# Scores of a windowed attention from stacked rows through memory, halves straight from PSUM, reciprocals in PSUM

## The reference

```python
x = x + jnp.tanh(g_xattn[0]) * attention(_layernorm(x), ctx, ctx, wq, bq, wk, bk, wv, bv, wo, bo)
x = x + jnp.tanh(g_ffn[0]) * experts(_layernorm(x), ln_gamma, ln_beta, Wr, W12, W3)
```

```python
q = split(jnp.einsum('btc,oc->bto', query, wq) + bq) * SCALE      # SCALE = 16 ** -0.5
k = split(jnp.einsum('btc,oc->bto', key, wk) + bk)
scores = jnp.where(valid, jnp.einsum('bhnrd,bhncd->bhnrc', qb, kc), neg_inf)
out = jnp.einsum('bhnrc,bhncd->bhnrd', softmax(scores), vc)
```

## Time and profile before

| | before |
|---|---|
| median of 3 runs | 534.16 us (533.97 to 535.27) |
| profiled execution | 534.19 us |
| its span in the trace | 532.3 us |
| granted TensorE clock, mean | 0.973 |
| busy in the span: TensorE, VectorE, ScalarE, GpSimd | 90%, 68%, 56%, 39% |

### The profile page before, as it was taken

The page is one execution under the profiler, slowest core; times in us unless marked ns, Lnnn a source line. Parts: engine busy times, 40 slices in busy tenths (PEclk is TensorE's granted clock), DMA queues, the critical chain, the costliest instruction groups (busy, mean ns, idle before and its releaser), DMA issues.

```text
span 532.3 us, 10749 instructions
## 1 busy us (share of the span) xinstructions
PE 479.7 (90%) x3551; PEld 444.7 (84%) x3551; DVE 360.8 (68%) x854; ACT 298.9 (56%) x757; POOL 208.9 (39%) x272
## 2 busy tenths in 40 slices
PE   5699999899999877369998999999999999999991
PEld 4588887777877666269998999999999999999991
DVE  6867888988888997547876574485843768544240
ACT  3689878677778764416664564373723747423230
POOL 8636776787787566510212012203032030311202
PEclk9999999999999997779999999999999999999996
DMA  8868432314142611153677362347451474201111
GB/s 269 209 140 250 78 41 72 75 57 81 42 80 55 205 42 53 58 175 118 234 184 219 78 226 34 60 129 193 132 144 20 130 188 131 31 4 17 13 19 20
DMA packets 41649, 57.33 MB, mean 108 GB/s; under 512 B 3721, under 2 KB 38576, under 8 KB 39552
## 3 DMA queue, kind: packets, MB, share of 16 engines
q1 hardware_dynamic: 35168, 48.62, 31.7%
q0 software_dynamic: 6144, 8.07, 9.1%
q10 hardware_dynamic: 288, 0.00, 0.0%
HBM read 36.24 MB, written 16.72 MB: 99 GB/s over the span
## 4 chain that ended last, share of the span: by engine, by line
PE 55%; DVE 3%; issue 2%; POOL 1%; DMA 0%; ACT 0%; POOLq 0%; DVEq 0%
PE bank L1438 17%; PE bank L1440 17%; PE bank L1439 17%; PE bank L1432 2%; PE bank L1361 1%; PE bank L1304 1%; POOL expert_rows L484 0%; DMA expert_rows<-xr,slotu 0%; DVE pT L929 0%; PE bank L1290 0%; POOL out_tokens L546 0%; DVE nm L924 0%; PE bank L1231 0%; PE bank L1238 0%; DVE osum L938 0%
## 5 line engine op out<-in xcount | busy, mean ns | idle before, releaser
L546 POOL DMA_INDIRECT out_tokens<-ysc,rows x32 | 49.6, 1550 | 245.6 <-DVE ysc L1142 238.9
L1438 PE MATMUL bank<-bXh,wh 128*128 128x384 f32 (+1 forms) x384 | 122.1, 318 | 2.9 <-issue 2.6
L1440 PE MATMUL bank<-bXh,wl 128*128 128x384 f32 (+1 forms) x384 | 121.8, 317 | 0.0
L1439 PE MATMUL bank<-bXl,wh 128*128 128x384 f32 (+1 forms) x384 | 121.8, 317 | 0.0
L749 ACT ACTIVATE sil<-bank 128x384 f32<-128x384 f32 (+1 forms) x96 | 43.7, 456 | 128.4 <-PE bank L1440 127.2
L1121 DVE TENSOR_TENSOR hF<-sil,bank 128x384 f32<-128x384 f32 (+1 forms) x96 | 48.9, 510 | 77.9 <-ACT sil L749 71.3
L633 ACT ACTIVATE p<-bank,nm 128x128 f32<-128x128 f32 x256 | 73.6, 387 | 14.7 <-DVE nm L924 14.7
L1438 PEld LDWEIGHTS bank<-bXh,wh 128*128 128x128 f32 x384 | 72.7, 189 | 3.3 <-issue 3.3
L1438 PE MATMUL bank<-wh,hH 128*128 128x256 f32 x256 | 73.8, 288 | 0.3 <-DVE ysc L1142 0.3
L1439 PEld LDWEIGHTS bank<-bXl,wh 128*128 128x128 f32 x384 | 72.7, 189 | 0.0
L1440 PEld LDWEIGHTS bank<-bXh,wl 128*128 128x128 f32 x384 | 72.6, 189 | 0.0
(11 more groups left out here) (146 smaller groups left out, 878.8 us busy)
## 6 DMA issues: line engine op xcount, KB each, us to landing
stage<-in_w12T SPq DMA_DIRECT2D x16, 1024.0 KB
stage<-in_w3T SPq DMA_DIRECT2D x8, 1024.0 KB
expert_rows<-padrow SPq DMA_DIRECT2D x8, 662.5 KB, 7.9
rows<-expert_rows SPq DMA_DIRECT2D x7, 662.5 KB, 4.4
kM<-k SPq DMA_DIRECT2D x64, 64.0 KB, 2.4
cT<-in_ctxT SPq DMA_DIRECT2D x8, 256.0 KB, 3.1
out_tokens<-x_all SPq DMA_DIRECT2D x8, 256.0 KB, 2.3
x_all<-in_x SPq DMA_DIRECT2D x2, 640.0 KB, 8.5
```

What stands on the lines that cost most here:

```text
L546: pool.indirect_dma_start(out=out, out_offset=bass.IndirectOffsetOnAxis(rows[par][:, c, D + E:ROW].bitcast(U32), 0), in_=ysc[par][:, c, :] ...
L1438: nc.tensor.matmul(out_ap, ah, bh, start=start, stop=False)
L1439: nc.tensor.matmul(out_ap, ah, bl, start=False, stop=False)
L1440: return nc.tensor.matmul(out_ap, al, bh, start=False, stop=stop)
```

## The change

Four things are changed.

The scores of blocks 1 to 7. The three products are put on top of each other in rows: two heads have 32 rows, and the three pairs of halves stand in 3 x 32 = 96 rows (qS holds queries high, high, low; kS keys high, low, high). Two heads are 256 columns, so a group is two products of 256 columns over 96 rows (`scores`). Block 0 keeps the old form (`first_scores`, one kM).

The way there. Queries and keys must change rows for that. SyncE stores each half into a scratch tensor in memory (qD, kD: four stores of 256 KB a block), waits for the store, and loads from there into the stacks: six loads of 128 KB into 16 rows for the keys, three of 256 KB into 32 rows for the queries (`stack`, in place of `spread_keys`). kS is cleared once, kS[0] by VectorE, kS[1] by GpSimd.

The halves. ScalarE writes the high half straight from PSUM with the bias added, VectorE the low half straight from PSUM (`keys_low`, `queries_low`: bank plus bias less the high half), so that kT, qT, two copies by ScalarE and two subtractions by GpSimd a block go. The scale of the queries goes to the copy of the input's columns. The bank Xp is handed on in another order: keys of the next block in step 0, columns of the input in step 1, queries in step 2, values in step 6. `normalize_inputs` of GpSimd comes ahead of the first normalization.

The reciprocals of the heads' sums are written into PSUM, behind the outputs of the heads (orec).

The core of the diff (changed lines only; renamed semaphores and small edits of the start are left out):

```diff
+        qD = nc.dram_tensor("query_halves", (2, P, DC, SB * T), F32).ap()
+        kD = nc.dram_tensor("key_halves", (2, P, DC, SB * T), F32).ap()
...
-        kM = [sb(pa, f"kM{i}", [P, 2, H, SB * T], F32R) for i in range(2)]
+        kM = sb(pa, "kM", [P, 2, H, SB * T], F32R)
+        kS = [sb(pa, f"kS{i}", [P, HP, 2, SB * T], F32R) for i in range(2)]
...
-        qT = sb(pa, "qT", [P, DC, SB * T], F32)
-        q2 = [sb(pa, f"q2_{i}", [P, 2, DC, SB * T], F32R) for i in range(2)]
-        kT = sb(pa, "kT", [P, DC, SB * T], F32)
+        qS = [sb(pa, f"qS{i}", [P, HP, SB * T], F32R) for i in range(2)]
+        q0 = qS[0][:, 0:2 * DC, :].rearrange("p (s c) t -> p s c t", s=2)
+        q2 = sb(pa, "q2", [P, 2, DC, SB * T], F32R)
...
-        orec = sb(pa, "orec", [P, 8], F32)
...
+        orec = [O[i][:, 8 * VW:8 * VW + 8] for i in range(2)]
...
-            def spread_keys(n, par):
-                sp.wait_ge(pool_kl, n + 1)
+            def spread_first_keys():
+                sp.wait_ge(dve_kl, 1)
-                    sp.dma_start(kM[par][r, :, a:H:HR, :].bitcast(F32), k2[r, :, :, :].bitcast(F32)).then_inc(ld_km[a // GH], 16)
+                    sp.dma_start(kM[r, :, a:H:HR, :].bitcast(F32), k2[r, :, :, :].bitcast(F32)).then_inc(ld_km[a // GH], 16)
+            def stack_keys(par, part, half):
+                for h in range(2):
+                    r = part * SR + h * HD
+                    sp.dma_start(kS[par][r:r + HD, :, h, :].bitcast(F32).rearrange("d (c a) t -> d c a t", c=DC),
+                                 kD[half].rearrange("(a h d) c t -> h d c a t", h=2, d=HD)[h]).then_inc(ld_k, 16)
+            def stack_queries(par, part, half):
+                sp.dma_start(qS[par][part * SR:(part + 1) * SR, :, :].bitcast(F32).rearrange("r (c a) t -> r c a t", c=DC),
+                             qD[half].rearrange("(a r) c t -> r c a t", r=SR)).then_inc(ld_q, 16)
+            def stack(n, par):
+                sp.wait_ge(act_kh, DC * (n + 1))
+                sp.dma_start(kD[0], k2[:, 0, :, :].bitcast(F32)).then_inc(sent_kh, 16)
+                sp.wait_ge(dve_kl, n + 1)
+                sp.dma_start(kD[1], k2[:, 1, :, :].bitcast(F32)).then_inc(sent_kl, 16)
+                sp.wait_ge(sent_kh, 16 * n)
+                stack_keys(par, 0, 0)
+                stack_keys(par, 2, 0)
+                sp.wait_ge(sent_kl, 16 * n)
+                stack_keys(par, 1, 1)
+                sp.wait_ge(act_qh, DC * (n + 1))
+                sp.dma_start(qD[0], q2[:, 0, :, :].bitcast(F32)).then_inc(sent_qh, 16)
+                sp.wait_ge(dve_ql, n + 1)
+                sp.dma_start(qD[1], q2[:, 1, :, :].bitcast(F32)).then_inc(sent_ql, 16)
+                sp.wait_ge(sent_qh, 16 * n)
+                stack_queries(par, 0, 0)
+                stack_queries(par, 1, 0)
+                sp.wait_ge(sent_ql, 16 * n)
+                stack_queries(par, 2, 1)
...
-            sp.wait_ge(km_zero[0], 4)
-            spread_keys(0, 0)
+            sp.wait_ge(km_zero, 3)
+            spread_first_keys()
-            sp.wait_ge(km_zero[1], 3)
-            spread_keys(1, 1)
+            sp.wait_ge(ks_zero[1], 1)
+            stack(1, 1)
...
-                spread_keys(n, par)
+                    sp.wait_ge(ks_zero[0], 2)
+                stack(n, par)
...
-            keys_low(0)
+            pool.memset(kS[1][:, :, :, :].bitcast(F32), 0.0).then_inc(ks_zero[1], 1)
...
-                if nxt:
-                    keys_low(n + 1)
+                if nxt2:
+                    normalize_inputs(n + 2)
-                if nxt2:
-                    normalize_inputs(n + 2)
-                if nxt:
-                    queries_low(n + 1, 1 - par)
...
-                act.activation(xT[:, :, :], Xp[:, :].rearrange("p (c t) -> p c t", c=DC), ACT.Copy).then_inc(act_xT, 1)
-            def queries(n, par, bank, prev1):
+                act.activation(xT[:, :, :], Xp[:, :].rearrange("p (c t) -> p c t", c=DC), ACT.Copy, scale=HD ** -0.5).then_inc(act_xT, 1)
+            def queries(n, halves, bank):
-                if prev1:
-                    act.wait_ge(pool_ql, n)
+                if not (isinstance(n, int) and n < 2):
+                    act.wait_ge(sent_qh, 16 * (n - 1))
-                    act.activation(qT[:, t, :], bank[:, t * SB * T:(t + 1) * SB * T], ACT.Identity,
-                                   bias=bq4[:, t:t + 1], scale=HD ** -0.5).then_inc(act_q32, 1)
-                act.wait_ge(act_q32, DC * (n + 1))
-                act.activation(q2[par][:, 0, :, :], qT[:, :, :], ACT.Copy).then_inc(act_q, 1)
-            def keys(n, bank, prev1):
+                    act.activation(halves[:, 0, t, :], bank[:, t * SB * T:(t + 1) * SB * T], ACT.Identity, bias=bq4[:, t:t + 1])\
+                       .then_inc(act_qh, 1)
+            def keys(n, bank):
-                if prev1:
-                    act.wait_ge(pool_kl, n)
+                if isinstance(n, int) and n == 1:
+                    for half in ld_km:
+                        act.wait_ge(half, KM)
+                elif not isinstance(n, int) or n > 1:
+                    act.wait_ge(sent_kh, 16 * (n - 1))
-                    act.activation(kT[:, t, :], bank[:, t * SB * T:(t + 1) * SB * T], ACT.Identity, bias=bqkv[:, 1, t:t + 1])\
-                       .then_inc(act_k32, 1)
-                if prev1:
-                    for half in ld_km:
-                        act.wait_ge(half, KM * n)
-                act.wait_ge(act_k32, DC * (n + 1))
-                act.activation(k2[:, 0, :, :], kT[:, :, :], ACT.Copy).then_inc(act_kT, 1)
+                    act.activation(k2[:, 0, t, :], bank[:, t * SB * T:(t + 1) * SB * T], ACT.Identity, bias=bqkv[:, 1, t:t + 1])\
+                       .then_inc(act_kh, 1)
...
+                    if g == 7 and nxt:
+                        values(n + 1, Xp)
+                    if cur:
+                        exps(G, g, not prev1 and g < 2)
+                    if g == 0 and nxt:
+                        keys(n + 1, Xp)
-                    if g == 7 and nxt:
-                        values(n + 1, Xp)
-                    if g == 3 and nxt:
-                        keys(n + 1, Xp, True)
-                    if cur:
-                        exps(G, g, not prev1 and g < 2)
-                    if g == 4 and nxt:
-                        queries(n + 1, 1 - par, Xp, True)
-                    if g == 0 and nxt:
+                    if g == 2 and nxt:
+                        queries(n + 1, q2, Xp)
+                    if g == 1 and nxt:
...
-            keys(0, K0, False)
+            act.wait_ge(ident_ok, 1)
+            act.activation(kM[:, 1, :, :].rearrange("p h (a t) -> p (h a) t", t=P),
+                           ident32[:, :].unsqueeze(1).to_broadcast([P, 2 * H, P]), ACT.Copy, scale=0.0).then_inc(km_zero, 1)
+            keys(0, K0)
-            queries(0, 0, Q0, False)
-            act.activation(kM[1][:, 1, :, :].rearrange("p h (a t) -> p (h a) t", t=P),
-                           ident32[:, :].unsqueeze(1).to_broadcast([P, 2 * H, P]), ACT.Copy, scale=0.0).then_inc(km_zero[1], 1)
+            queries(0, q0, Q0)
...
-                dve.reciprocal(orec[:, :], ob[:, :, 3 * HD]).then_inc(dve_rec, 1)
+                dve.reciprocal(orec[k % 2], ob[:, :, 3 * HD]).then_inc(dve_rec, 1)
-                                  orec[:, :].unsqueeze(2).to_broadcast([P, 8, HD]), ALU.mult).then_inc(dve_on, 1)
+                                  orec[k % 2].unsqueeze(2).to_broadcast([P, 8, HD]), ALU.mult).then_inc(dve_on, 1)
...
+            def keys_low(n, bank):
+                if isinstance(n, int) and n == 1:
+                    for half in ld_km:
+                        dve.wait_ge(half, KM)
+                elif not isinstance(n, int) or n > 1:
+                    dve.wait_ge(sent_kl, 16 * (n - 1))
+                dve.wait_ge(act_kh, DC * (n + 1))
+                for t in range(DC):
+                    ins = dve.scalar_tensor_tensor(k2[:, 1, t, :], bank[:, t * SB * T:(t + 1) * SB * T], bqkv[:, 1, t:t + 1],
+                                                   k2[:, 0, t, :].bitcast(F32), ALU.add, ALU.subtract)
+                ins.then_inc(dve_kl, 1)
+            def queries_low(n, halves, bank):
+                if not (isinstance(n, int) and n < 2):
+                    dve.wait_ge(sent_ql, 16 * (n - 1))
+                dve.wait_ge(act_qh, DC * (n + 1))
+                for t in range(DC):
+                    ins = dve.scalar_tensor_tensor(halves[:, 1, t, :], bank[:, t * SB * T:(t + 1) * SB * T], bq4[:, t:t + 1],
+                                                   halves[:, 0, t, :].bitcast(F32), ALU.add, ALU.subtract)
+                ins.then_inc(dve_ql, 1)
...
+                    if g == 1 and nxt:
+                        keys_low(n + 1, Xp)
+                    elif g == 3 and nxt:
+                        queries_low(n + 1, q2, Xp)
...
-                    pe.wait_ge(act_vf, n)
+                    pe.wait_ge(dve_kl, n + 1)
...
```

(50 more changed lines are left out.)

43 lines of the change are left out of this document (21 added, 22 removed).

## The result

The changed kernel took 548.32 us (median of four runs, 546.99 to 549.24) beside 534.47 for the kernel before: a ratio of 1.0247, 95% interval 1.0214 to 1.028. It is slower by 13.9 us, where 6 us less was forecast, and lies above the range.

The account below looks back on a forecast made before the run. TensorE was taken to bound blocks 1 and 2, a GpSimd-VectorE circle of 24.0 us blocks 3 to 6. Terms +7.4 + 1.0 - 2.0 - 10.5 - 2.2 = -6.3 us took 534.19 to 528, range 519 to 541.

Parts of the forecast that it names:

- the circle of waits: In blocks 3 to 6, GpSimd's 12.3 us and VectorE's 11.7 make the 24.0 us period, to become 21.9.
- The start of block 2: Block 2's scores wait behind padding and the scratch round trip, starting near 67 us against 59.65: +7.4 us.
- The chain: Block 2's scratch round trip: queries land 10.5 to 14.5 us after the key store has landed at 53 to 56.
- The clock: TensorE, idle some 6 us before block 2, gets a dip of its granted clock: +1.0 us (0 to 2).
- Block 2: VectorE, with new operations from PSUM, becomes the bound; block 2 goes from 22.4 to 20.4 us: -2.0.
- Blocks 3 to 6: Four middle attention blocks go from 24.3 to 21.7 us each, 86.8 for four: -10.5 us.
- both had slack: In blocks 3 to 6 ScalarE and GpSimd had slack, so taking halves from PSUM alone moves nothing.
- Block 7: Last attention block, without new halves, goes from 23.7 to 21.5 us: -2.2.
- Scores, scaling, new operations: In attention blocks: score group 0.47 us for 0.92, scaling of heads 0.3 to 0.35, VectorE's four new operations 0.47 each.
- The expert stage: The stage after 236 us, which the change doesn't touch; no term in the sum.
- (a): The round trip through memory sets the period, about 23.5 us a block in blocks 3 to 6: +8.3, 542.5 us; chance 0.18.
- (b): Blocks 3 to 6: reciprocals in PSUM fail or the wait moves to small operations; 23.2 a block, +1.9, 536 us; chance 0.20.

Follow-up runs that it names:

- two products: Changed kernel without the scores' third product (low queries with high keys): 64 stacked rows for 96, fewer scratch transfers; 544.77 us, ratio 1.0177.
- the run that was kept running: Changed kernel with dummy transposes on TensorE, 20 ahead of block 1's first scores and 60 ahead of block 2's; 540.47 us, ratio 1.0072.
- the idle waits: Changed kernel with 40 and 120 already met waits on TensorE ahead of the first scores of blocks 1 and 2; 549.22 us, ratio 1.0268.
- the 50 dummies: Changed kernel with 50 dummy transposes on TensorE where it waits for the first expert's rows; 543.70 us, ratio 1.0156.
- the exponentials first: Changed kernel with ScalarE's first exponentials and block 1's keys ahead of the values' copy in block 0; 549.25 us, ratio 1.0246.
- padding moved: Changed kernel with the second padding stores and the zero-row store issued by GpSimd after block 0, not by SyncE; 549.76 us, ratio 1.0257.
- the kernel with 50 dummies: Kernel before with reciprocals in PSUM, first exponentials ahead of the values' copy, 50 dummy transposes before the first expert; 531.04 us, ratio 0.991.
- the one with 20: Kernel before with reciprocals in PSUM, first exponentials ahead of the values' copy, 20 dummy transposes before the first expert; 527.76 us, ratio 0.9858.

## Why the prediction was wrong

The sum came out 21.5 us too low: 5.6 in blocks 3 to 6, 5.2 in the start of block 2, 4.8 in the expert stage, 3.1 in block 2 with the clock, 2.3 in block 7 and 0.5 behind it. The largest is the circle of waits in blocks 3 to 6, told below; the third is a stage that the sum had at nothing.

**The start of block 2** (predicted +7.4, was +12.6): the mechanism was right, padding and round trip ahead of block 2's scores, and two sizes were off. Block 1 began at 44.2, for 41 to 43. The chain was counted as 10.5 to 14.5 us from a landed key store and took 14.9, since key loads ran at 137 GB/s with the DMA engines full, as the earlier trace rows had it (0.74 at 105), and next to the query stores; the store had landed at 57.6, for 53 to 56. The experiment with two products shows that the amount counts: four transfers less a turn and a shorter chain gave 2.8 and 4.2 us. That the padding stood in SyncE's own queue is worth 0.7; what its 3.3 MB cost as such no run shows. The Trainium skill ("SBUF — State Buffer", section "Door 1: The DMA port swizzle") gives 104 GB/s for 16 partitions and so spoke against the change; the trace agrees in direction, in the start rather than in the steady blocks, and can't test the figure, since the 137 GB/s measured include query stores from 128 partitions.

**The clock** (+1.0): it cost 2.4 us in block 2, by the run that was kept running. TensorE stood still for 6.84 us, and 0.50 lasted ten; the term was sized by a milder dip in the earlier trace rows. Two more falls of 3.5 us, at 27.0 and 44.0, lie in the +12.6.

**Block 2** (-2.0, was -0.3 or less without the clock: 24.5 - 2.4 = 22.1 for 22.38, or 22.4 between the first scores in the run that was kept running): VectorE, which was to be its bound, was not full there (17.4 of 24.5). What held it isn't shown.

**Blocks 3 to 6** (-10.5, was -4.9, with the clock at 1.00 on both sides): this is the step that failed. The circle was read as GpSimd's 12.3 and VectorE's 11.7. Its first half was right. Its second half was TensorE's as well: the profile before had 11.69 of 12.26 us of TensorE there, and the prediction didn't cut its window so.

```profile
106.74:118.63 11.89, 10.59 (x85) 8.93 (x84) 10.23 (x28) 9.16 (x27) 9.57 (x13) 1.00 0.16 55
118.63:130.89 12.26, 11.69 (x99) 9.78 (x100) 10.97 (x31) 9.49 (x29) 9.44 (x13) 1.00 0.47 84
```

The same two halves in the changed kernel:

```profile
119.66:132.71 13.05, 11.20 (x96) 9.60 (x94) 10.71 (x29) 11.50 (x32) 10.61 (x14) 1.00 0.48 135
132.71:142.75 10.04, 8.19 (x86) 6.91 (x87) 9.27 (x34) 6.49 (x22) 5.88 (x9) 1.00 0.88 209
```

The second half went to 10.04, near the forecast's 9.6, which took both the reciprocals and the shorter scores: the reciprocals alone left it at 11.86. The first half grew from 11.89 to 13.05. There ScalarE now has 11.50 us of work for 9.16, since the high halves of keys and queries (0.86 and 0.84) moved into it from the second, and TensorE stands 1.09 us for `oT` and 0.75 for the context, both in the steps up to 3. Over the four blocks the wait for GpSimd's values, with which the circle closed, is gone (4.2 us before), and in its place TensorE waits 14.3 us: 7.3 for ScalarE's `oT`, 3.5 for VectorE's clipped logits, 1.8 for its choice of experts, 1.1 for the context, 0.6 for queries. The prediction costed the moved steps at nothing, with "both had slack". Which of these waits decides isn't settled: reordering only exchanged them.

A profile of these blocks must be read with its clock. With the changed kernel's code in them the four blocks took 92.9 us in all four executions in which the clock stood at 1.00 throughout (the changed kernel, the idle waits, the 50 dummies, the exponentials first), and 95.3 and 96.2 in two (padding moved, kept running) in which it fell to 0.50 twice, for 3.5 us each time. In the kernel before with reciprocals in PSUM and exponentials first it was 94.8 twice at 1.00 and 96.6 with one fall. No single long wait stands ahead of these falls, and what sets them off no run shows: ahead of the one at 93.2 us in the kernel with 50 dummies TensorE was busy for 5.66 of 7.0 us (86 to 93), and in the one with 20, where none came, for 5.56 of the same seven.

**Block 7** (-2.2, was +0.1): nothing of the gain shows; the clock fell to 0.50 for 3.5 us in it (from 194.2; 0.93 in the mean), and before it fell only behind the block, at 203.2. No run was made for it.

**Scores, scaling, new operations**: right. From a group's start to its transposes 0.45 us (119.66 to 120.11) for 0.47; scaling 0.29; VectorE's new operations 0.47 to 0.48 each; VectorE's clash with the clearing 2.69 us for two normalizations (1.69 in the earlier trace rows).

**The expert stage** (0, was +4.8): "which the change doesn't touch" was true of its source and not of where its code lies. The stalls make 5.5 us for 2.6, and the clock's fall behind the second some 1.6 more. A third of the loss is this.

**The rivals.** (a) came nearest (+8.3 for +13.9), for a wrong reason: in blocks 3 to 6 only 0.18 and 0.60 us of two blocks' scores waited for queries. (b) holds in one half: in the kernel before the reciprocals bring nothing, in the changed one some 4 us.

## What to carry over

A circle of waits is closed by every engine that is full in one of its parts: cut the windows at the circle's own turning points and read each part, before giving a part to one engine. Transfers that replace work on a chip that is already moving its weights are paid where the DMA engines are full, at the start, and what waits for them also loses its clock. And a few microseconds may lie in where unchanged code ends up: look for stalls without a releaser in the parts that a change doesn't touch, and shift the code before calling a small difference an effect. Look at the granted clock of a window before comparing it with another: one fall of 3.5 us moved a block by 0.8 to 1.9 us here.

## What the runs showed of the hardware

- Stalls of TensorE of 1.6 to 3.1 us that no work in the profile accounts for, at three fixed places of a stage of unchanged code, each at a jump; 20 dummy transposes ahead took one away (297.0 to 292.7 us), 50 moved it to another place.
- The granted clock fell to 0.50 for 3.5 us in some executions and not in others, with the same code and nearly the same work of TensorE ahead (block 3 with 50 and with 20 dummies: 25.9 and 24.0 us).
- Products of 64 rows between work of 128 rows had the loading of weights idle 0.23 us ahead of nearly each pair; products of 96 rows hadn't.
- VectorE's scaling of a tile in SBUF takes 286 to 290 ns whatever GpSimd does, once one input is in PSUM, for up to 3716 ns with both in SBUF; for the engine that sets the pace this may be worth nothing.
- Loads into 16 partitions, with query stores beside them, fill the DMA engines (share 1.00) at 137 GB/s, padding stores at 288 (share 1.11).
